# Head pair 0's K and V made during the layer norm of the keys, with other PSUM banks for Q and a norm cut into eight units

## The chip, the cores and the metric

The kernel runs on all 8 cores of one Trainium2 chip. Two cores share one of the 4 batch entries; each of the two owns half of its 4096 query rows and reads all 4096 key rows. No core sends anything to another. The metric is the device time of the slowest core in microseconds (us).

## The reference

All of it for x of shape [4, 4096, 1024], 16 heads of 64 columns, and a feed-forward layer with 3072 hidden columns and int weights:

```python
xn = _layernorm(x)
q = split_heads(xn @ Wq) + pos; k = split_heads(xn @ Wk) + pos; v = split_heads(xn @ Wv)
scores = einsum('bhqd,bhkd->bhqk', q, k) / sqrt(1024)     # causal mask, then softmax
s = (softmax(scores) @ v, heads merged) @ Wo
g = silu(down(silu(gate(xn)) * up(xn)))                    # weights int * 1/127
out = x + s * g
```

## The kernel before

The program is written engine by engine. `P.op` (line 142) appends one operation to the list of its engine, with the semaphore counts that it waits for; `P.flush` (line 150) closes a block. Each engine carries out its own list strictly in the order of the calls, so the order in which Python emits operations is the order on every engine. The engines are T (TensorE), V (VectorE), S (ScalarE), G (GpSimd, which issues the weight loads) and SY (SyncE, which issues the x loads). DVE in the profile is VectorE, ACT is ScalarE.

The blocks are: b0, the layer norm of the own query rows; f1 and f2, the feed-forward layer; b34, the layer norm of the 32 key tiles of 128 rows and the Q projection; b5, K, V and attention for 8 pairs of heads; b6, the output projection. The change touches b34 and b5.

**b34.** `ln_phase` (line 270) handles tile n as a chain. VectorE sums x (line 301), ScalarE squares it (304), VectorE sums the squares (307), small operations follow on both (310 to 328), and VectorE writes the normed tile (332). TensorE transposes it with 8 matmuls (347) and ScalarE copies the result into `xn_kv` (354). Then `interleave_cb(n)` may emit other work, which lies in every engine's list ahead of tile n+1. In the kernel before, `b4_cb` (627) emits the Q projection of pair p, `emit_qpair(p)` (575), after tile n = 16 + 2p. It has four groups, one for each 512 query rows: 8 matmuls into `Qps` (595, two banks in turn), position added (602), square (607), a matmul with a column of ones into `SQp1` (611), and a maximum over it (619). A group's ones matmul lies in TensorE's list ahead of the next group's 8 matmuls.

**b5.** `kv_units(p)` (687) returns the preparation of pair p as 43 units: one that issues the loads of Wk and Wv (696, 701); 8 K units, `emit_kg` (8 matmuls at 715, evacuated at 723, banks `KVp[0]` and `KVp[1]` in turn); one norm unit, `u_norms`, which goes over all 8 groups of K with one scratch buffer `sSQ` (square 740, ones matmul 747, maximum 753, running maximum 763); 32 V units, `emit_vc` (8 matmuls at 779 for 128 keys, evacuated at 787); and `u_bound` (798), which turns the maxima into the exponential's bias `sBM` (VectorE 800 to 810, matmul 816, VectorE 825). Pair 0's units are all emitted ahead of its attention (965).

`attention(p)` (837) has four query blocks j with 8, 16, 24 and 32 key chunks c. Chunk c is: two matmuls into `SC2[c % 2]` (851), one exponential of 128 x 1024 on ScalarE (865), for the last 4 chunks of a block two multiplications with the triangle (878), and, emitted two chunks later, two matmuls into `AVps` (897). After every odd chunk, and once after the block's last AV matmuls, one unit of pair p+1 is taken from the list `fillers` (911, 915). I call these places slots: 5 + 9 + 13 + 17 = 44 in a pair. What is left in the list is emitted after the last block (962). At the end of a block ScalarE inverts the sums (922, 929), TensorE spreads them into `KVp` (936), and VectorE copies them (945) and scales the output (953).

Of the kernel before, what the change touches and what calls it, by code (L numbers as in the profile page):

```python
# [172 lines left out]
def build_program(cfg):  # L173
# [40 lines left out]
    with ExitStack() as top:  # L214
        P.mksem(top, "sT", "sS", "sV", "dC", "dX0", "dX1", "dW0", "dW1",
                "dS0", "dS1", "dG0", "dG1", "dR0", "dR1", "dR2", "dR3", "dO0", "dO1", "dP", "dK")
# [11 lines left out]
        b5set = 2 * S + 2 * KVC * 130 + 4 * EC * 128 + 2 * 2 * QBS + 512 + QBS  # L228
# [15 lines left out]
        o = 0  # L244
# [10 lines left out]
        sSQ = BIG1[:, o:o + 512]  # L255
        o += 512
# [13 lines left out]
        def ln_phase(xt_src, ntile, xn_dst, dsem, gates, tag, pool_ext=None,  # L270
                     xnt_ext=None, xnt_gate=None,
                     tp_gate=None, sq_gate=None, interleave_cb=None):
            with ExitStack() as ph:
# [3 lines left out]
                else:  # L277
# [5 lines left out]
                Tps = [pe(nc.psum_tensor(f"Tps{tag}{i}", [128, GT * 128], F32))  # L283
                       for i in range(2)]
                sqb = pe(nc.psum_tensor(f"sqb{tag}", [128, E], F32))
# [8 lines left out]
                for n in range(ntile):  # L294
# [64 lines left out]
                    if interleave_cb is not None:  # L359
                        interleave_cb(n)  # L360
                return last_ev, tile_toks

        with ExitStack() as phb0:
# [178 lines left out]
            with ExitStack() as phc:  # L542
# [3 lines left out]
                sPQ = Kp[0][:, 0:OWN]  # L546
# [17 lines left out]
                with ExitStack() as ph4:  # L564
                    p4 = ph4.enter_context
                    Qps = [p4(nc.psum_tensor(f"Qps{i}", [128, QW], F32))
                           for i in range(2)]
                    SQp1 = p4(nc.psum_tensor("SQp1", [1, QW], F32))
                    wq_free = [None, None]
                    qps_free = [None, None]  # L570
                    b4st = dict(sqmm_free=None, sqb_free=tok_f2T)
                    tok_mq = [None] * NP
                    qbs_per_qs = max(1, 4 // NQW)

                    def emit_qpair(p):
                        par = p % 2
                        dsem = "dS0" if par == 0 else "dS1"
                        tw = P.op("G", lambda g, o=Wsl[par][:],
                                  s=wqr[:, :, p * 128:(p + 1) * 128]:
                                  g.dma_start(out=o, in_=s),  # L580
                                  waits=[wq_free[par], tok_f2T], inc=dsem, amt=16)
                        rlast = None
                        for qs in range(NQW):
                            qp = qs % 2
                            last = None
                            for ec in range(EC):
                                w = [tw, tok_xnown, qps_free[qp]]
                                if p == 0 and qs == 0 and ec == 0:
                                    w += [tok_f2S, tok_f1V]
                                last = P.op(  # L590
                                    "T", lambda t, o=Qps[qp][:],
                                    l=Wsl[par][:, ec, :],
                                    r=xn_own[:, ec, qs * QW:(qs + 1) * QW],
                                    st=(ec == 0), sp=(ec == EC - 1):
                                    t.matmul(o, l, r, start=st, stop=sp),
                                    waits=w, inc="sT" if ec == EC - 1 else None)
                            wq_free[par] = last
                            tev = P.op("V", lambda v,
                                       o=Q_all[:, p, qs * QW:(qs + 1) * QW],
                                       a=Qps[qp][:],  # L600
                                       b=sPQ[:, qs * QW:(qs + 1) * QW]:
                                       v.tensor_tensor(o, a, b, ALU.add),
                                       waits=[last, tpq], inc="sV")
                            qps_free[qp] = tev
                            tsq = P.op("V", lambda v, o=sSQ[:, 0:QW],
                                       a=Q_all[:, p, qs * QW:(qs + 1) * QW]:
                                       v.tensor_tensor(o, a, a, ALU.mult),
                                       waits=[tev, b4st["sqb_free"]], inc="sV")
                            tmm = P.op("T", lambda t, o=SQp1[0:1, 0:QW],
                                       l=sONE[:], r=sSQ[:, 0:QW]:  # L610
                                       t.matmul(o, l, r, start=True, stop=True),
                                       waits=[tsq, tok_consts,
                                              b4st["sqmm_free"]], inc="sT")
                            b4st["sqb_free"] = tmm
                            for jj in range(qbs_per_qs):
                                j = qs * qbs_per_qs + jj
                                rlast = P.op(
                                    "V", lambda v, p=p, j=j, jj=jj:
# [8 lines left out]
                    def b4_cb(n):  # L627
                        if n >= 16 and (n - 16) % 2 == 0 and (n - 16) // 2 < NP:
                            emit_qpair((n - 16) // 2)
# [453 lines left out]
```

How the kernel before makes its waits and increments, by code:

```python
            def body(eng):  # L152
                hw = self.hw[qn]
                for fn, waits, inc, amt in ops:
                    for (sn, val) in waits:
                        if val > hw.get(sn, 0):
                            eng.wait_ge(self.sems[sn][0], val)
                            hw[sn] = val
                    ins = fn(eng)
                    if inc is not None:
                        ins.then_inc(self.sems[inc][0], amt)
```

## Time and profile before

| | |
|---|---|
| median of 3 runs | 2590.89 us (2503.78 to 2601.6) |
| profiled execution, its own time | 2503.69 us |
| its span, first to last instruction | 2502.1 us |
| spans of the 8 cores in it | 2495.4 to 2502.1 us |
| TensorE (PE) busy | 1716.1 us, 69% |
| VectorE (DVE) busy | 827.2 us, 33% |
| ScalarE (ACT) busy | 956.7 us, 38% |
| b34, from the first key tile's load | 752 to 1114 us |
| K and V of pair 0 ahead of the attention | 1114 to 1180 us |
| attention of 8 pairs | 1180 to 2353 us |
| output projection | 2353 to 2502 us |

A timeline row gives the start in us from the span's start, the length in us, the engine, the line and the operation; in brackets stands how long the engine had been idle before it and whose result ended that. PEld rows (weight loads) lie beside the PE rows. The granted clock is 1.0 at 2.4 GHz and 0.5 at 1.2 GHz.

### The profile page before, as it was taken

The numbers are of one execution on the slowest core, as the hardware profiler recorded it, in microseconds if no ns is written. First come the engines' busy times: TensorE is split into PE (matmuls) and PEld (weight loads), VectorE is DVE, ScalarE is ACT, GpSimd is POOL, SyncE is SP. The second block draws the span as 40 slices with busy tenths as digits, with TensorE's granted clock in tenths as the row PEclk, the third lists the DMA queues.
The fourth block names the chain that finished last, engine by engine and source line by source line (L and its number), as shares of the span: only waits on it lengthen the run. The fifth ranks groups of instructions, "written<-read, shape, count | busy, mean of one in ns | idle before, by whom it ended". The sixth has DMA issues, their size and how long they took to land. (4 is left out here: it accounts for less than half of the span.)

```text
span 2502.1 us, 26111 instructions; the slowest of 8 cores (2495.4 to 2502.1 us)
## 1 busy us (share of the span) xinstructions
PE 1716.1 (69%) x8995; PEld 706.8 (28%) x9088; DVE 827.2 (33%) x1746; ACT 956.7 (38%) x1125; POOL 87.4 (3%) x135
## 2 busy tenths in 40 slices
PE   1178888989991144437787787878877697776753
PEld 0134444444440111114232232323222232221221
DVE  4533333330005544434413323232332423321133
ACT  3311111111003311110485675747657475677500
POOL 0011101000000000000000000000000000000000
PEclk9999999999995576678898888978888888888886
DMA  2153433320114221220000000000000000020155
GB/s 77 59 64 39 51 39 45 44 26 30 54 52 109 76 51 42 42 33 10 5 1 9 1 5 5 5 5 1 5 5 5 1 1 1 1 34 1 51 176 176
DMA packets 75135, 89.85 MB, mean 36 GB/s; under 512 B 52994, under 2 KB 53122, under 8 KB 74882
## 3 DMA queue, kind: packets, MB, share of 16 engines
q0 software_dynamic: 62768, 45.62, 11.7%
q1 hardware_dynamic: 12242, 42.57, 5.3%
q8 instruction: 77, 1.26, 0.2%
q14 instruction: 48, 0.39, 0.1%
HBM read 100.24 MB, written 16.78 MB: 47 GB/s over the span
## 5 line engine op out<-in xcount | busy, mean ns | idle before, releaser
L865 ACT ACTIVATE BIG<-SC,sBM 128x1024 bf16<-128x1024 f32 x640 | 681.9, 1110 | 343.7 <-PE SC L851 343.2
L897 PE MATMUL AVps<-BIG 128*65 128x512 bf16 x1280 | 425.6, 414 | 87.3 <-DVE BIG L878 42.0
L851 PE MATMUL SC<-BIG 64*128 64x512 bf16 x1280 | 265.0, 420 | 0.0
L485 ACT ACTIVATE sSG<-Gps 128x512 bf16<-128x512 f32 x96 | 57.3, 597 | 378.5 <-PE Gps L471 378.5
L787 DVE CAST BIG<-KVp 128x128 bf16<-128x128 f32 x256 | 75.0, 293 | 375.1 <-PE KVp L779 372.3
L471 PE MATMUL Gps<-RA,wgT 128*128 128x512 bf16 x752 | 195.5, 405 | 1.4 <-issue 0.7
L481 PE MATMUL Ups<-RA,wuT 128*128 128x512 bf16 x744 | 180.6, 382 | 1.3
L779 PE MATMUL KVp<-BIG 128*128 128x128 bf16 x2048 | 167.8, 230 | 13.5 <-DVE BIG L945 13.1
L897 PEld LDWEIGHTS AVps<-BIG 128*65 128x65 bf16 x1280 | 104.4, 114 | 235.2 <-issue 224.5
L347 PE MATMUL Tpsb<-sID,BIG 128*128 128x128 bf16 x256 | 32.4, 306 | 200.1 <-DVE BIG L332 200.1
L525 PE MATMUL Dps<-BIG 128*128 128x512 bf16 x752 | 165.1, 379 | 2.2 <-PEq L164 1.4
L490 DVE TENSOR_TENSOR BIG<-sSG,Ups 128x512 bf16<-128x512 bf16 x96 | 66.0, 687 | 283.5 <-PE Ups L481 279.0
L878 DVE TENSOR_TENSOR BIG<-BIG,sTRI 128x512 bf16<-128x512 bf16 x256 | 97.3, 421 | 174.8 <-ACT BIG L865 174.8
L779 PEld LDWEIGHTS KVp<-BIG 128*128 128x128 bf16 x2048 | 126.0, 102 | 77.4 <-issue 73.5
L715 PE MATMUL KVp<-BIG 128*128 128x512 bf16 x489 | 131.3, 415 | 23.3 <-DMA BIG<-Wv 11.0
L851 PEld LDWEIGHTS SC<-BIG 64*128 64x128 bf16 x1280 | 59.7, 94 | 268.2 <-issue 268.2
L471 PEld LDWEIGHTS Gps<-RA,wgT 128*128 128x128 bf16 x768 | 77.5, 102 | 94.4 <-issue 16.4
L322 ACT ACTIVATE sLN<-sLN,sCV 128x1 f32<-128x1 f32 x48 | 14.1, 294 | 235.0 <-DVE sLN L319 235.0
L481 PEld LDWEIGHTS Ups<-RA,wuT 128*128 128x128 bf16 x768 | 76.2, 99 | 95.0 <-issue 7.8
L525 PEld LDWEIGHTS Dps<-BIG 128*128 128x128 bf16 x768 | 75.1, 98 | 92.2 <-issue 1.8
L1025 PE MATMUL OPs<-BIG,RA 128*128 128x512 bf16 x250 | 71.4, 450 | 37.7 <-DVE ot L1042 33.3
L747 PE MATMUL KVp<-BIG,sONE 128*1 128x512 bf16 x64 | 32.6, 510 | 90.1 <-DVE BIG L740 90.1
(79 smaller groups left out, 1292.9 us busy)
## 6 DMA issues: line engine op xcount, KB each, us to landing
xstA<-x_q SPq DMA_DIRECT2D x32, 512.0 KB, 4.4
xstb<-x_kv SPq DMA_DIRECT2D x32, 512.0 KB, 3.6
g_spill<-xstA POOLq DMA_DIRECT2D x16, 512.0 KB, 2.9
gt<-g_spill POOLq DMA_DIRECT2D x16, 512.0 KB, 6.0
out<-ot SPq DMA_DIRECT2D x16, 512.0 KB, 3.0
wgc<-wg POOLq DMA_DIRECT2D x24, 256.0 KB, 4.1
wuc<-wu POOLq DMA_DIRECT2D x24, 256.0 KB, 5.6
wdc<-wd POOLq DMA_DIRECT2D x24, 256.0 KB, 5.7
```

The lines of the kernel that those rows point to most:

```text
L471: t.matmul(o, l, r, start=st, stop=sp),
L481: t.matmul(o, l, r, start=st, stop=sp),
L490: v.tensor_tensor(o, a, b, ALU.mult),
L525: t.matmul(o, l, r, start=st, stop=sp),
L715: t.matmul(o, l, r, start=st_, stop=sp),
L779: t.matmul(o, l, r, start=st_, stop=sp),
L787: v.tensor_copy(o, i_),
L851: t.matmul(SC2[bi][:, h * QBS:(h + 1) * QBS], Kp[par][h * 64:(h + 1) * 64, c * 128:(c + 1) * 128], Q_all[h * 64:(h + 1) * 64, p, j * QBS:( ...
L865: s.activation(expb[bi], SC2[bi][:], AF.Exp, scale=cfg.SM, bias=sBM[par][:, col:col + 1]),
L878: v.tensor_tensor(expb[bi][:, h * QBS:(h + 1) * QBS], expb[bi][:, h * QBS:(h + 1) * QBS], sTRI[:, r * QBS:(r + 1) * QBS], ALU.mult),
L897: t.matmul(AVps[h][:], Vaug[par][:, c, h, :], expb[bi][:, h * QBS:(h + 1) * QBS], start=st_, stop=sp),
L1025: t.matmul(OPs[op][:, ew * EW:(ew + 1) * EW], AO[:, rc, q2 * 128:(q2 + 1) * 128], Wo_sb[:, rc, ew * EW:(ew + 1) * EW], start=st_, stop=sp),
```

## The change

1. The PSUM tensors of attention (`SC2`, `AVps`, `KVp`) are now allocated ahead of b34. b34 uses them: the transposes go to `SC2[1]`, the squares of the layer norm to `AV2`, the Q matmuls to the first bank of `SC2[0]`, the Q ones matmul to its second. So Q has one bank instead of two, and it is marked free only after the maximum (619 before).
2. Q of pair p is emitted after tile 2p instead of 16 + 2p.
3. The units of pair 0 are emitted inside b34, each after the tile that completes its input: the loads after tile 0, V unit c after tile c, K unit g and the norm of its group after tile 4g + 3, the bound at the end. The callback emits at most three units for one tile. Pair 0's weights go to slices 2 and 3 of `Wsl`, so that they don't collide with Wq.
4. `u_norms` is cut into 8 units, and `sSQ` has two halves. With one empty unit, `u_setk`, a pair has 1 + 8 + 1 + 8 + 32 + 1 = 51 units instead of 43. The loop over slots is as before.
5. K/V loads count on semaphores of their own (`dV0`, `dV1`), and `sPQ` lies in another part of `Kp[1]`.

```diff
-                sPQ = Kp[0][:, 0:OWN]
+                sPQ = Kp[1][:, 2 * E:2 * E + OWN]
...
+                Qps = [SC2[0][:, 0:QW]]
+                SQp1 = SC2[0][0:1, 512:512 + QW]
...
+                        qp = 0
...
+                        b4st["sqmm_free"] = rlast
+                        qps_free[qp] = rlast
...
+                def kv_units(p, ks, vs, xw):
...
+                    units.append((0, u_dma))
...
+                    for kg_ in range(NKG):
+                        units.append(((kg_ + 1) * TPK - 1,
+                                      lambda kg_=kg_: emit_kg(kg_)))
...
+                    units.append((NKG * TPK - 1, u_setk))
+
+                    def u_norm1(kg):
+                        sqi = kg % 2
+                        tsq = P.op("V", lambda v, sqi=sqi,
+                                   o=sSQ[sqi][:, 0:KW],
+                                   a=Kp[par][:, kg * KW:(kg + 1) * KW]:
+                                   v.tensor_tensor(o, a, a, ALU.mult),
+                                   waits=[st["kvb"][kg % 2],
+                                          sqst["free"][sqi], kv["ktok"]],
+                                   inc="sV")
...
+                    for kg_ in range(NKG):
+                        units.append(((kg_ + 1) * TPK - 1,
+                                      lambda kg_=kg_: u_norm1(kg_)))
...
+                    for c_ in range(KVC):
+                        units.append((c_, lambda c_=c_: emit_vc(c_)))
...
+                    units.append((KVC - 1, u_bound))
...
+                b34q = [(2 * p_, lambda p_=p_: emit_qpair(p_))
+                        for p_ in range(NP)]
+                holder = {}
+                b34q += kv_units(0, 2, 3, lambda r: holder["toks"][r])
+                b34q.sort(key=lambda it: it[0])
...
+                def b34_cb(n, toks):
+                    holder["toks"] = toks
+                    c = 0
+                    while (qpos[0] < len(b34q) and b34q[qpos[0]][0] <= n
+                           and c < 3):
+                        b34q[qpos[0]][1]()
+                        qpos[0] += 1
+                        c += 1
...
+                    tps_ext=[SC2[1][:, 0:GT * 128],
+                             SC2[1][:, GT * 128:2 * GT * 128]],
+                    sqb_ext=AV2[:, 0:E],
...
-                    for u in kv_units(0):
-                        u()
                     for p in range(NP):
                         if p + 1 < NP:
-                            fillers.extend(kv_units(p + 1))
+                            fillers.extend(
+                                fn for _, fn in kv_units(
+                                    p + 1, (p + 1) % 2, 2 + (p + 1) % 2,
+                                    lambda r: tok_xnkv))
                         attention(p)
```

## Rows read from the trace of the kernel before

**Rows 1.** The page's granted clock in 40 slices, and its costliest group
```profile
PEclk9999999999995576678898888978888888888886
...
L865 ACT ACTIVATE BIG<-SC,sBM 128x1024 bf16<-128x1024 f32 x640 | 681.9, 1110 | 343.7 <-PE SC L851 343.2
```

**Rows 2.** Timeline, one layer-norm tile: start us, length us, engine, line, operation, [idle before]
```profile
826.30 1.01 PE L347 MATMUL Tpsb<-sID,BIG 128*128 128x128 bf16 x8 [5.90 <-DVE BIG L332]
826.98 1.07 ACT L354 CAST BIG<-Tpsb 128x512 bf16<-128x512 f32 x2 [2.24 <-PE Tpsb L347]
...
829.09 1.23 DVE L307 TENSOR_REDUCE sLN<-sqbb 128x1 f32<-128x1024 f32 x1 [1.91 <-ACT sqbb L304]
...
833.21 1.01 PE L347 MATMUL Tpsb<-sID,BIG 128*128 128x128 bf16 x8 [5.90 <-DVE BIG L332]
```

**Rows 3.** Timeline of the Q projection: two groups at the higher clock, one at the lower
```profile
880.45 1.90 PE L595 MATMUL Qps<-RA,BIG 128*128 128x512 bf16 x8
880.62 0.68 DVE L619 TENSOR_REDUCE sMQ<-SQp 1x1 f32<-1x512 f32 x1 [0.63 <-PE SQp L611]
...
892.28 1.20 DVE L301 TENSOR_REDUCE sLN<-xstb 128x1 f32<-128x1024 f32 x1
...
970.77 3.20 PE L595 MATMUL Qps<-RA,BIG 128*128 128x512 bf16 x8
```

**Rows 4.** Tile 0: timeline row of its transposes, and the Wq loads of line 580
```profile
763.95 1.01 PE L347 MATMUL Tpsb<-sID,BIG 128*128 128x128 bf16 x8 [17.51 <-DVE BIG L332]
...
L580 POOL DMA_DIRECT2D BIG<-Wq x8: 873/873/901, 754.0 to 1043.4; - x8
...
DMA to landing us min/median/max: 4.2/4.6/19.1
```

**Rows 5.** Timeline from the last layer-norm tile to the first attention exponential
```profile
1112.80 1.07 ACT L354 CAST BIG<-Tpsb 128x512 bf16<-128x512 f32 x2 [2.17 <-PE Tpsb L347]
...
1124.18 2.72 PE L715 MATMUL KVp<-BIG 128*128 128x512 bf16 x6 [11.04 <-DMA BIG<-Wv]
...
1127.64 0.69 DVE L723 TENSOR_TENSOR BIG<-KVp,sPK 128x512 bf16<-128x512 f32 x1 [15.78 <-PE KVp L715]
...
1156.26 20.28 PE L779 MATMUL KVp<-BIG 128*128 128x128 bf16 x256
...
1176.86 0.21 DVE L800 TENSOR_SCALAR sMK<-sMQ,sMK 1x4 f32<-1x4 f32 x1
...
1179.52 1.28 ACT L865 ACT_TABLE_LOAD   x1 [65.65 <-DVE sBM L825]
```

**Rows 6.** Timeline of the norm unit that lies in the attention of pair 2
```profile
1517.58 2.12 ACT L865 ACTIVATE BIG<-SC,sBM 128x1024 bf16<-128x1024 f32 x2 [1.34 <-PE SC L851]
...
1521.58 0.41 DVE L740 TENSOR_TENSOR BIG<-BIG 128x512 bf16<-128x512 bf16 x1
...
1522.13 0.38 PE L747 MATMUL KVp<-BIG,sONE 128*1 128x512 bf16 x1 [1.59 <-DVE BIG L740]
1522.68 0.68 DVE L753 TENSOR_REDUCE sMK<-KVp 1x1 f32<-1x512 f32 x1 [0.70 <-PE KVp L747]
...
1535.00 1.11 ACT L865 ACTIVATE BIG<-SC,sBM 128x1024 bf16<-128x1024 f32 x1 [15.30 <-PE SC L851]
...
1536.54 1.11 ACT L865 ACTIVATE BIG<-SC,sBM 128x1024 bf16<-128x1024 f32 x1 [0.42 <-PE SC L851]
```

**Rows 7.** Timeline: an ordinary stretch of slots, a masked chunk, the end of a pair
```profile
1610.18 2.12 ACT L865 ACTIVATE BIG<-SC,sBM 128x1024 bf16<-128x1024 f32 x2 [0.19 <-PE SC L851]
...
1621.57 0.76 DVE L878 TENSOR_TENSOR BIG<-BIG,sTRI 128x512 bf16<-128x512 bf16 x2 [0.25 <-ACT BIG L865]
...
1626.54 0.24 PE L816 MATMUL KVp<-sBSB,sOR 1*128 1x1 bf16 x4 [3.14 <-DVE sBSB L810]
...
1632.08 1.40 DVE L945 CAST BIG<-KVp 64x512 bf16<-64x512 f32 x2 [4.50 <-PE KVp L936]
1632.67 2.12 ACT L865 ACTIVATE BIG<-SC,sBM 128x1024 bf16<-128x1024 f32 x2 [1.44 <-PE SC L851]
```

More of the change, by code:

```diff
@@ L254, in build_program @@
         o += 2 * 2 * QBS
-        sSQ = BIG1[:, o:o + 512]
-        o += 512
+        sSQ = [BIG1[:, o:o + 512], BIG1[:, o + 512:o + 1024]]
+        o += 1024
         sRS = BIG1[:, o:o + QBS]
@@ L271, in ln_phase @@
                      xnt_ext=None, xnt_gate=None,
-                     tp_gate=None, sq_gate=None, interleave_cb=None):
+                     tp_gate=None, sq_gate=None, interleave_cb=None,
+                     tps_ext=None, sqb_ext=None):
             with ExitStack() as ph:
@@ L282, in ln_phase @@
                         for i in range(2)]
-                Tps = [pe(nc.psum_tensor(f"Tps{tag}{i}", [128, GT * 128], F32))
-                       for i in range(2)]
-                sqb = pe(nc.psum_tensor(f"sqb{tag}", [128, E], F32))
+                Tps = tps_ext if tps_ext is not None else [
+                    pe(nc.psum_tensor(f"Tps{tag}{i}", [128, GT * 128], F32))
+                    for i in range(2)]
+                sqb = sqb_ext if sqb_ext is not None else pe(
+                    nc.psum_tensor(f"sqb{tag}", [128, E], F32))
                 xst_free = [None, None]
@@ new lines, in build_program @@
+                SC2W = max(2 * QBS, 2 * GT * 128, 2 * QW)
+                SC2 = [pc(nc.psum_tensor(f"SC2_{i}", [128, SC2W], F32))
+                       for i in range(2)]
+                AVPD = max(QBS, 512)
+                KVPD = max(KW, 512)
+                AV2 = pc(nc.psum_tensor("AV2", [128, max(2 * AVPD, E)], F32))
+                KV2 = pc(nc.psum_tensor("KV2", [128, max(2 * KVPD, E)], F32))
+                AVps = [AV2[0:65, 0:QBS], AV2[0:65, AVPD:AVPD + QBS]]
+                KVp = [KV2[:, 0:KW], KV2[:, KVPD:KVPD + KW]]
@@ new lines, in build_program @@
+                tok_xnkv, _ = ln_phase(
+                    xkv_t, ntile_kv, xn_kv, ("dX0", "dX1"),
+                    [tok_f1T, tok_f1V], "b",
+                    xnt_ext=[Kp[1][:, i * E:(i + 1) * E]
+                             for i in range(2)],
+                    xnt_gate=tok_f2T,
+                    tp_gate=tok_f2S, sq_gate=tok_f1V,
+                    tps_ext=[SC2[1][:, 0:GT * 128],
+                             SC2[1][:, GT * 128:2 * GT * 128]],
+                    sqb_ext=AV2[:, 0:E],
+                    interleave_cb=b34_cb)
@@ L655, in build_program @@
+                while qpos[0] < len(b34q):
+                    b34q[qpos[0]][1]()
+                    qpos[0] += 1
+                tok_b4T = P.cnt("sT")
+                tok_b4V = P.cnt("sV")
+                tok_b4S = P.cnt("sS")
+                P.flush("b34")
                 tok_Q = tok_b4V
+                st["sc2"] = [tok_Q, tok_b4S]
+                st["av_free"] = [tok_Q, tok_Q]
+                st["sl_free"][0] = tok_b4T
+                st["sl_free"][1] = tok_b4T
                 with ExitStack() as ph5:
```

467 lines of the change are left out of this document (214 added, 253 removed).

## The prediction

> **What bounds the kernel now.** I read the page first. ScalarE's exponential is the costliest group and ScalarE waited 344 us for the scores, so in attention ScalarE is starved at some places; and the granted clock falls to 0.5 for two slices and stays at 0.6 to 0.7 for four more, from the key layer norm to the start of attention [rows 1]. Then I read timelines of single periods, because the two blocks have different limits.
>
> In b34 nothing is busy enough to be the limit: a plain tile takes 6.91 us (transposes at 826.30 and at 833.21) and is one chain over three engines. The sum of squares (line 307) starts at 829.09, and the chain runs on from there; ahead of it TensorE and VectorE have gaps [rows 2]. In attention a slot of two chunks keeps ScalarE idle for only 0.19 us per 2.12 us of exponentials [rows 7]. One unit breaks this: the norm unit. Each of its 8 groups is square, ones matmul, maximum in turn through one scratch buffer; TensorE stands in it, no scores come, and ScalarE is idle for 15.3 us [rows 6]. It occurs in 7 pairs' attention. Ahead of attention K and V of pair 0 run alone: from the last copies' end (1112.80 + 1.07 = 1113.87) to the first exponential (1179.52 + 1.28 = 1180.80) it is 66.9 us, 11.0 of them a wait for Wv [rows 5].
>
> **The change in b34.** Emission order is execution order, so what a unit makes VectorE wait for lies ahead of tile n+1's sums.
>
> Removed: the 66.9 us, less what must still follow tile 31. That is K group 7 (start to evacuation 3.5 us, evacuation 0.7 [rows 5]), its square 0.4, ones matmul to maximum 0.6, maximum 0.7 [rows 6], V unit 31 with evacuation 1.2, and the bound from 1176.86 to 1180.80, 3.9 [rows 5]. With hand-overs about 11.5 us. Gain 55.
>
> Tile 0: Q of pair 0 now follows tile 0. Its matmuls would start at about 765.2; but Wq, issued at 754.0 behind the loads of the positions, landed after 19.1 us, at 773.1 [rows 4]. Cost 8 us. Sixteen tiles of layer norm covered this before. Bounds 0 (if it lands as the median load, 4.6 us) and 12 (if Wk and Wv, now behind it, slow it down).
>
> One Q bank: group q+1 started at 880.45, while the maximum of group q ran from 880.62 to 881.30 [rows 3]. Now it starts behind the maximum, at about 881.4: 0.93 us later, three times in a pair, 8 pairs: 22 us. The longer gap also bears on the clock. The same 8 matmuls took 1.90 us at 2.4 GHz and 3.20 at 1.2 GHz [rows 3]; a slow group moves what follows by 1.5 us. Of 24 later groups 3 were slow before. I take 1.3 more in each pair, 8 x 2 = 16 us; bounds 0 and, if all are slow, 36.
>
> V units: in 16 tiles with nothing else (n = 1, 5, ... and the even ones from 16) the copies end at 828.05 [rows 2]. The V unit takes 8 matmuls at 1.2 GHz, to about 829.1, and its evacuation 0.3, to 829.45. The sum of x, 1.2 us long [rows 3], used to lie beside the transposes and now comes after, and the sum of squares starts at 830.55 instead of 829.09: 1.45 us each, 23 us. Bounds 0 (if VectorE had room) and 35. In the 8 Q tiles only the end of the V unit sticks out behind the last maximum, 0.5 us: 4.
>
> K units with their norm, 7 tiles (the eighth is in the tail above): K matmuls from 828.15, evacuation at 831.7, square from 832.5, maximum 833.7 to 834.4, V unit evacuated by 834.9 or, where V waits for the bank of that maximum (odd groups), 835.8. The sum of squares starts at 836.0 or 836.9, 6.9 or 7.8 late: 51 us.
>
> Sum for b34: 8 + 22 + 16 + 23 + 4 + 51 - 55 = +69 us.
>
> The Trainium skill (page "TensorE: Matmul & The Clock Gate", on engine queue depths) says that ScalarE and VectorE are strict first-in first-out and that only TensorE lets weight loads pass. The trace agrees: in Q tiles the sum of x starts only at 892.28, behind the last maximum. If VectorE could pass a waiting evacuation, the V and K terms, 78 us, would go; that is the second rival below.
>
> **The change in attention**, for each of the 7 pairs with fillers.
>
> The norm unit goes: 15.3 us of idle, less the 0.19 of an ordinary slot, plus 0.7 because the next exponentials came 1.54 us apart instead of 1.1 while the clock recovered [rows 6, 7]: -15.8.
>
> Eight norm units take slots 11 to 18, which had V units. The square of the next group can run while TensorE does other chunks, so most cost nothing. Three are different. In slots 12 and 13 (masked chunks 13 and 15 of block 1) the square lies behind the mask of the same chunk, which starts about 1.6 us after the exponentials' pair and lasts 0.76 [rows 7]: TensorE waits, and the AV matmuls behind it come about 1.7 and 1.2 us later. In slot 15 the square lies behind copies and scalings of 1.40 us each: 1.3. Less 0.5 for the V units that were there: +3.7. Bounds 0 and 8.
>
> The bound left slot 43, where TensorE waited 3.14 us [rows 7]; a V unit is there now (20.28 us for 32, 0.63 each [rows 5]), and a part of the wait lay beside masks: -2.1.
>
> Fifty-one units don't fit in 44 slots. Six V units and the bound are left and come after the pair, with ScalarE idle, since the next pair's exponentials need the bias. The V units wait for `KVp`, copied from 1632.08 to 1633.48; six units and their first evacuation behind the scalings take until 1638.8; the bound without its table load 2.7: 1641.5, against an exponential at 1632.67 [rows 5, 7]. 8.9, less 0.8 as the first AV matmul no longer waits for the scaling: +8.1. If the clock is low, 10 or 11.
>
> Sum: -15.8 + 3.7 - 2.1 + 8.1 = -6.1 us, seven times: -43. Bounds -9 and -3 each: -63 and -21. Pair 1's Wk and Wv are issued only after b34, but their first use is some 7 us later and a load takes about 5: nothing, at most 4.
>
> **Sum.** +69 - 43 = +26 us on the profiled execution's 2503.7 (span 2502.1): about 2530 us. That execution is at the low end of the three runs, whose median is 2590.9; I predict on its footing. About 2% (50 us, so 2454 to 2554) is what a measurement of this kernel can tell from no change.
>
> **Rivals.**
>
> *The clock stays low (slower).* If every gap of some 2.5 us drops TensorE to 1.2 GHz, all later Q groups are slow (+20 over my sum) and the end of each pair runs slow (+3 x 7): 2573 us. For it: one pair's second group was slow with gaps of only 1.8 us, and the layer norm runs at 0.5 [rows 1, 3]. Against: most groups with such gaps ran at 1.90. It decides from two slow groups a pair on. The Trainium skill has a rule that speaks for it (the same page, "A second HAM failure mode: psum-queue depth-cycling"): small idles between matmul groups that wait for PSUM make the clock swing, and throughput falls.
>
> *The layer norm hides the units (faster).* If VectorE's gaps in b34 take in the evacuations, the 78 us go and -50 remains: 2452 us. For it: VectorE and TensorE are mostly idle there. Against: list order, and the 892.28 row. It decides if over 75 of the 78 go.
>
> *The norm units stall anyway (slower).* If each of the 8 stands 1.9 us for its square, 15 us a pair, attention gains nothing: +11.3 x 7 on my sum, 2609 us. Against: a square takes 0.41 us and VectorE is idle in unmasked slots.
>
> **Chances.** Forecast, within 2%: 0.70. Low clock 0.18, stalls 0.05: slower 0.23. Hidden units 0.07: faster. The range takes the bounds: the Q clock 0 to 36, the V units, and -63 to -21 for attention. The low ends seldom meet: 2494 to 2575.
>
> **What would show it.** Right: layer-norm tiles of 8.4 us with V only and about 14 with K; Q of pair 0 starting at about 773; ones matmuls at even spacing in the slots and no 15 us idle of ScalarE; 8 to 9 us idle of it at each pair's end; first exponential near 1250 instead of 1181; pair periods 6 us shorter. Wrong: V-only tiles still at 6.9, or norm units with TensorE waits of over 1 us in unmasked slots.

## The result, and the profile after

| | kernel before | changed kernel |
|---|---|---|
| median | 2508.12 us (8 runs) | 2574.55 us (8 runs, 2572.91 to 2577.23) |
| ratio of the times | | 1.0274, 95% interval 1.0262 to 1.0287 |
| spans of the 8 cores in the profiled execution | 2495.4 to 2502.1 us | 2561.1 to 2575.5 us |
| TensorE (PE) busy | 69% | 69% |
| core 0: transposes of tile 0 to those of tile 31 | 759.7 to 1108.0 us | 763.75 to 1254.78 us |
| core 0: first and last exponential | 1175.3, 2345.5 us | 1269.33, 2419.7 us |
| core 0: attention between them | 1170.3 us | 1150.4 us |

The change costs 2.7%. The forecast was 1% more and "within 2%". From here on all rows and numbers are of core 0, unless another core is named. It is the slowest core of the changed kernel; before it was the fastest one, and core 6, whose rows the prediction used, the slowest. So the change is 80.1 us on core 0 (2495.4 to 2575.5), 62.0 us on core 6 (2502.1 to 2564.1) and 66.4 us between the medians: differences of core 0 overstate it. In some executions the cores of one die ran at a lower granted clock and took some per cent longer; the ratios in this document leave these out, and so do the times of "norm in one unit" and "pair 0's K and V behind", of which two executions each are left.

The page of the changed kernel, its granted clock in 40 slices of 64.4 us and its costliest group:

```profile
PEclk9999999999985655555589798888889788888886
...
L903 ACT ACTIVATE BIG<-SC,sBM 128x1024 bf16<-128x1024 f32 x640 | 683.9, 1111 | 321.8 <-PE SC L889 257.5
```

TensorE stood at or near 0.5 from slice 13 to slice 20, which is from 773 to about 1290 us, where before only two slices stood at 0.5 [rows 1]. In attention ScalarE waits less, 321.8 us instead of 342.4 (core 0 of before). So the attention gained and b34 lost, as forecast; the sizes differ. The windows view of b34, before and changed (its columns: the stretch, its length, the busy time and the number of instructions of PE, PEld, DVE, ACT and POOL, the granted clock, the DMA share, GB/s):

```profile
759.70:1108.00 348.30, 116.69 (x529) 53.00 (x538) 174.97 (x344) 77.57 (x155) 5.24 (x6) 0.66 0.22 53
...
763.00:1255.00 492.00, 207.78 (x837) 89.70 (x851) 195.94 (x404) 77.61 (x155) 5.24 (x6) 0.55 0.17 39
```

The granted clock is 0.55 where it was 0.66. Timeline rows of two layer-norm tiles of the changed kernel, one with a V unit only, one with a K unit, its norm and a V unit:

```profile
804.53 1.01 PE L350 MATMUL SC<-sID,BIG 128*128 128x128 bf16 x8 [5.38 <-DVE BIG L335]
...
807.54 0.29 DVE L772 CAST BIG<-KV 128x128 bf16<-128x128 f32 x1 [3.16 <-PE KV L765]
807.75 1.21 DVE L304 TENSOR_REDUCE sLN<-xstb 128x1 f32<-128x1024 f32 x1
...
812.82 1.01 PE L350 MATMUL SC<-sID,BIG 128*128 128x128 bf16 x8 [5.38 <-DVE BIG L335]
...
1137.95 1.01 PE L350 MATMUL SC<-sID,BIG 128*128 128x128 bf16 x8 [5.38 <-DVE BIG L335]
...
1151.80 1.01 PE L350 MATMUL SC<-sID,BIG 128*128 128x128 bf16 x8 [6.07 <-DVE BIG L335]
```

Transposes to transposes it is 8.29 us with V only (6.91 before, [rows 2]) and 13.85 us with K. The list order of VectorE is to be read at 807.54: the evacuation of the V unit waits for TensorE, and the sum of x (line 304) starts only behind it, though ScalarE began to square the same x at 806.17, 1.6 us earlier. Timeline rows of Q groups, the first in tile 0 and others:

```profile
772.80 3.57 PE L605 MATMUL SC<-RA,BIG 128*128 128x512 bf16 x8 [8.04 <-DMA BIG<-Wq]
...
778.61 0.68 DVE L631 TENSOR_REDUCE sMQ<-SC 1x1 f32<-1x512 f32 x1 [0.84 <-PE SC L623]
...
779.43 3.57 PE L605 MATMUL SC<-RA,BIG 128*128 128x512 bf16 x8 [0.93 <-DVE sMQ L631]
...
875.74 1.89 PE L605 MATMUL SC<-RA,BIG 128*128 128x512 bf16 x8 [0.93 <-DVE sMQ L631]
...
900.60 3.44 PE L605 MATMUL SC<-RA,BIG 128*128 128x512 bf16 x8 [0.93 <-DVE sMQ L631]
```

Q of pair 0 starts at 772.80, behind an 8.04 us wait for Wq. In every later group of a pair TensorE stands idle for 0.93 us, from the ones matmul to the end of the maximum. One of these groups, at 875.74, took 1.89 us. The others shown took 3.57 and 3.44; of the 24 later groups 23 took 2.69 us or more. The median of one matmul is 631 ns where it was 380. The groups view of TensorE between 763 and 1256 us (count, busy us, mean ns of one matmul, idle us before them and who ended it):

```profile
L605 PE MATMUL SC<-RA,BIG 128*128 128x512 bf16 x248 | 104.4, 594 | 31.2 <-DVE sMQ L631 22.3 <-DMA BIG<-Wq 8.0 <-issue 0.9
...
L623 PE MATMUL SC<-BIG,sONE 128*1 128x512 bf16 x32 | 16.4, 514 | 49.1 <-DVE BIG L618 49.1
```

The same view of before has 74.3 us, 452 ns and 1.8 us of idle time for its Q matmuls. So the Q matmuls took 30.1 us more, waited 22.3 us for the maxima and 8.0 us for Wq. Timeline rows from the last tile to the attention:

```profile
1254.78 1.01 PE L350 MATMUL SC<-sID,BIG 128*128 128x128 bf16 x8 [5.38 <-DVE BIG L335]
...
1269.33 2.12 ACT L903 ACTIVATE BIG<-SC,sBM 128x1024 bf16<-128x1024 f32 x2
...
1278.21 3.57 PE L688 MATMUL KV<-BIG 128*128 128x512 bf16 x8 [4.52 <-DMA BIG<-Wv]
```

14.55 us lie between the last tile's transposes and the first exponential, where before it was 67.3 (1108.0 to 1175.3). The first K unit of the attention then waits 4.52 us for Wv, and ScalarE, behind it, is idle for 8.37 us. Timeline rows of three of the eight norm units of one pair:

```profile
1609.19 0.42 DVE L716 TENSOR_TENSOR BIG<-BIG 128x512 bf16<-128x512 bf16 x1
...
1609.76 0.38 PE L723 MATMUL KV<-BIG,sONE 128*1 128x512 bf16 x1 [2.56 <-DVE BIG L716]
...
1611.25 1.11 ACT L903 ACTIVATE BIG<-SC,sBM 128x1024 bf16<-128x1024 f32 x1 [2.83 <-PE SC L889]
...
1615.25 0.58 PE L723 MATMUL KV<-BIG,sONE 128*1 128x512 bf16 x1 [2.56 <-DVE BIG L716]
...
1624.75 0.59 PE L723 MATMUL KV<-BIG,sONE 128*1 128x512 bf16 x1 [2.64 <-DVE BIG L716]
...
1626.97 1.11 ACT L903 ACTIVATE BIG<-SC,sBM 128x1024 bf16<-128x1024 f32 x1 [3.07 <-PE SC L889]
...
1632.67 0.38 PE L723 MATMUL KV<-BIG,sONE 128*1 128x512 bf16 x1
```

The norm matmuls of slots 12, 13 and 15 wait 2.56, 2.56 and 2.64 us for their squares, and ScalarE stands idle for 2.83 and 3.07 us behind the first and the third; behind the second it waits in front of the block's end, which these rows do not show. Slots 12 and 13 lie beside masked chunks, slot 15 behind the copies and scalings of the block before. The one at 1632.67, in a slot with neither, waits for nothing. Timeline rows of two pairs' ends:

```profile
1412.71 4.80 PE L765 MATMUL KV<-BIG 128*128 128x128 bf16 x48 [1.72 <-DVE BIG L984]
...
1420.44 2.12 ACT L903 ACTIVATE BIG<-SC,sBM 128x1024 bf16<-128x1024 f32 x2 [10.07 <-PE SC L889]
...
1567.04 2.12 ACT L903 ACTIVATE BIG<-SC,sBM 128x1024 bf16<-128x1024 f32 x2 [10.12 <-DVE sBM L810]
```

Six V units in one go (48 matmuls, 4.80 us), then the bound, and ScalarE idle for 10.07 us where it was 1.44 [rows 7]. The pair's period is 1567.04 - 1420.44 = 146.60 us; before it was 150.2 (seven pairs in 1051.4 us; now in 1031.3).

### The profile page after: what moved, and what is told of

It is laid out like the page before. It is cut to its first block and busy times, and to the rows that moved or that the text cites. A ratio compares the mean times of both kernels' runs of the same rounds, so it can differ in the third digit from the quotient of the medians.

```text
span 2575.5 us, 26000 instructions; the slowest of 8 cores (2561.1 to 2575.5 us)
## 1 busy us (share of the span) xinstructions
PE 1779.6 (69%) x8992; PEld 730.4 (28%) x9088; DVE 828.8 (32%) x1746; ACT 958.9 (37%) x1125; POOL 87.4 (3%) x135
## 5 line engine op out<-in xcount | busy, mean ns | idle before, releaser
L903 ACT ACTIVATE BIG<-SC,sBM 128x1024 bf16<-128x1024 f32 x640 | 683.9, 1111 | 321.8 <-PE SC L889 257.5
L936 PE MATMUL AV<-BIG 128*65 128x512 bf16 x1280 | 422.0, 413 | 86.6 <-DVE BIG L917 36.3
L765 PE MATMUL KV<-BIG 128*128 128x128 bf16 x2048 | 182.8, 245 | 37.1 <-DVE BIG L984 19.0
L772 DVE CAST BIG<-KV 128x128 bf16<-128x128 f32 x256 | 75.2, 294 | 362.3 <-PE KV L765 361.7
L936 PEld LDWEIGHTS AV<-BIG 128*65 128x65 bf16 x1280 | 102.9, 115 | 239.8 <-issue 230.0
L765 PEld LDWEIGHTS KV<-BIG 128*128 128x128 bf16 x2048 | 141.6, 110 | 97.7 <-issue 94.5
L688 PE MATMUL KV<-BIG 128*128 128x512 bf16 x486 | 145.9, 450 | 25.0 <-ACT BIG L357 9.0
L350 PE MATMUL SC<-sID,BIG 128*128 128x128 bf16 x256 | 32.4, 306 | 185.4 <-DVE BIG L335 185.4
L605 PE MATMUL SC<-RA,BIG 128*128 128x512 bf16 x248 | 104.4, 594 | 31.2 <-DVE sMQ L631 22.3
L695 DVE TENSOR_TENSOR BIG<-KV,sPK 128x512 bf16<-128x512 f32 x64 | 44.2, 690 | 191.9 <-PE KV L688 191.8
```

The costliest lines, as they stand in the source:

```text
L688: t.matmul(o, l, r, start=st_, stop=sp),
L765: t.matmul(o, l, r, start=st_, stop=sp),
L772: v.tensor_copy(o, i_),
L903: s.activation(expb[bi], SC2[bi][:, 0:2 * QBS], AF.Exp, scale=cfg.SM, bias=sBM[par][:, col:col + 1]),
L936: t.matmul(AVps[h][:], Vaug[par][:, c, h, :], expb[bi][:, h * QBS:(h + 1) * QBS], start=st_, stop=sp),
```

## Experiments

All ran beside the kernel before. "First exponential" is its start, "attention" the time from there to the start of the last exponential, both on core 0 of the profiled execution.

| kernel | median us | ratio to before, 95% interval | first exponential us | attention us |
|---|---|---|---|---|
| changed kernel | 2574.55 | 1.0274 (1.0262 to 1.0287) | 1269.3 | 1150.4 |
| Q bank freed earlier | 2504.75 | 0.998 (0.994 to 1.001) | 1196.6 | 1144.6 |
| gaps filled | 2531.28 | 1.008 (1.004 to 1.012) | 1222.0 | 1145.8 |
| norm in one unit | 2598.5 | 1.034 (1.024 to 1.044) | 1268.1 | 1174.2 |
| seven more slots | 2515.39 | 1.002 (0.999 to 1.005) | 1265.5 | 1084.2 |
| pair 0's K and V behind | 2537.0 | 1.013 (1.011 to 1.016) | 1230.6 | 1148.7 |
| norm units moved | 2527.91 | 1.009 (1.008 to 1.011) | 1262.7 | 1102.8 |
| all three repairs | 2412.80 | 0.963 (0.961 to 0.965) | 1206.4 | 1055.8 |
| b34 laid out anew | 2208.91 | 0.882 (0.880 to 0.884) | 1006.9 | 1047.1 |

### The wait for the maximum, and the clock

One line is taken out, so that the Q bank is free again once its sum has been evacuated. This is what the changed kernel's first release already said; the second one overwrote it.

```diff
-                        qps_free[qp] = rlast
```

> The changed kernel with one line less: the Q bank is free after the evacuation and no longer only after the maximum. In the changed kernel 1 of 24 later Q groups ran its 8 matmuls in 1.9 us; the others took 2.7 to 3.6. Theory A (the 0.93 us wait also keeps the clock low): the wait goes, 24 x 0.93 = 22 us, and most later groups return to 1.9 us, another 20 to 30: 45 us less than the changed kernel, about 2530. Theory B (the clock is low for another reason, such as the V units or the early place of Q): only 22 us go, about 2552, and the groups stay at 3 us and more.

The groups view of TensorE in b34, and then timeline rows, both of this kernel:

```profile
L605 PE MATMUL SC<-RA,BIG 128*128 128x512 bf16 x248 | 71.3, 437 | 5.5 <-DMA BIG<-Wq 4.9 <-issue 0.4
...
L623 PE MATMUL SC<-BIG,sONE 128*1 128x512 bf16 x32 | 12.2, 383 | 48.5 <-DVE BIG L618 48.5
```

```profile
872.47 1.90 PE L605 MATMUL SC<-RA,BIG 128*128 128x512 bf16 x8
872.64 0.68 DVE L631 TENSOR_REDUCE sMQ<-SC 1x1 f32<-1x512 f32 x1 [0.63 <-PE SC L623]
...
876.15 1.90 PE L605 MATMUL SC<-RA,BIG 128*128 128x512 bf16 x8
```

The group at 872.47 now starts 0.17 us ahead of the maximum, right behind the ones matmul, instead of after 0.93 us of idle TensorE, and takes 1.90 us; so do 23 of the 24 later groups. The Q matmuls take 71.3 us instead of 104.4, the 32 ones matmuls 12.2 instead of 16.4, and no time goes into waiting for maxima. The granted clock of b34 is 0.66, as before the change. Sum: 33.1 + 4.2 + 22.3 = 59.6 us; another 6 come from shorter V matmuls (27.5 instead of 30.4 us) and Wq (4.9 instead of 8.0). The tiles span 423.2 us instead of 491.0, 67.8 less. One line is thus worth 70 us of the total, more than I had expected (45), since the clock took more than I had put down for it. Theory B is out: the early place of Q and the V units are as before, and the groups are fast.

The same wait with no idle time in it tells whether the wait itself or TensorE's idleness brings the low clock. This kernel adds matmuls whose result is not used: four between a Q group and its ones matmul, three between that and the next group.

```diff
                         sqi = qs % 2
+                        for _d in range(4):
+                            P.op("T", lambda t: t.matmul(
+                                KVp[1][:, 0:KW], sID[:], xn_own[:, 0, 0:KW],
+                                start=True, stop=True), waits=[...])
```

> The changed kernel, its waits kept, with 4 matmuls of 128 x 512 ahead of each Q ones matmul and 3 behind it; their results are not used (they go to a K/V bank that is free then). They fill TensorE's gaps of 1.47 and 0.93 us. Theory A (low clock because of idle gaps): later groups run in 1.9 us, the wait of 0.93 stays, 25 to 33 us less than the changed kernel, about 2545. Theory B (the groups are slow for another reason, such as the PSUM bank or the loads): groups stay slow and the added matmuls make it 0 to 20 us longer.

Timeline rows of this kernel:

```profile
876.69 1.03 PE L622 MATMUL KV<-RA,sID 128*128 128x512 bf16 x4
...
878.64 0.82 PE L633 MATMUL KV<-RA,sID 128*128 128x512 bf16 x3
...
879.64 1.89 PE L605 MATMUL SC<-RA,BIG 128*128 128x512 bf16 x8 [0.18 <-DVE sMQ L641]
```

TensorE now waits only 0.18 us at the maximum, and the next group takes 1.89 us. All Q matmuls take 69.0 us. All 24 later groups now take 1.89 us, and the granted clock of b34 is 0.69. The dependency is the same, and TensorE does 61 us more work in b34 (35.0 and 26.3 us for the added matmuls), yet the first exponential comes 47 us earlier. So the low clock came from the idle gaps, not from the wait on the bank as such. This kernel fills both gaps of a group, 1.47 us ahead of the ones matmul and 0.93 behind it; that the second alone makes the difference is shown by the kernel before this one, which has the first gap and fast groups.

### The units inside the layer norm

Pair 0's units, all but the loads, are emitted behind the layer norm again. Q stays as in the changed kernel.

```diff
-                b34q += kv_units(0, 2, 3, lambda r: holder["toks"][r])
-                b34q.sort(key=lambda it: it[0])
+                kv0 = [fn for _, fn in
+                       kv_units(0, 2, 3, lambda r: holder["toks"][r])]
+                b34q.insert(1, (0, kv0.pop(0)))
...
+                for fn in kv0:
+                    fn()
```

> The changed kernel with pair 0's K and V units emitted behind the layer norm, as in the kernel before, all but their two loads, which stay ahead (issued behind tile 0). Everything else of the change stays (one Q bank, the attention's units). The layer norm stage loses the V units of its 16 tiles without a Q pair (1.4 us each, 22 us), the 4 us of those that share a tile with a Q pair, and 7 K tiles at 7.2 us (51 us): 77 us. Behind it the units take what they took before, 66.9 us from the end of the layer norm, less about 11 us of waiting for Wv, which is now there, and less some 11 us of units that were in the tail anyway: 44 us. Theory A (units emitted into the layer norm delay it by nearly their own time, because VectorE goes through one list): the first exponential comes about 33 us earlier than in the changed kernel, near 1236 us on core 0, total near 2541. Rival (the units lie hidden inside the layer norm and the loss is all the Q groups'): the first exponential comes about 44 us later, near 1313, total near 2618.

Timeline rows of this kernel, the last tile and the first exponential:

```profile
1172.08 1.01 PE L350 MATMUL SC<-sID,BIG 128*128 128x128 bf16 x8 [5.90 <-DVE BIG L335]
...
1230.62 2.12 ACT L906 ACTIVATE BIG<-SC,sBM 128x1024 bf16<-128x1024 f32 x2
```

The tiles span 1172.08 - 760.3 = 411.8 us. Against the changed kernel's 491.0 the V and K units cost 79.2 us inside the layer norm; the sum had 78. Against the 348.3 of before, Q alone costs 63.5 us; the sum had 46. Behind the tiles it is 58.5 us to the first exponential. The kernel took 2534.07 and 2539.93 us, against 2541 expected. The rival (units hidden in the layer norm) had 2618 and is out. So placing the units in the tiles loses time by itself: 79.2 us of delay for 58.5 - 14.55 = 44 us saved behind. With the loads issued early, K and V behind the tiles take 58.5 us, 8.8 less than before. The Q groups are slow here too (23 of the 24 later ones took more than 2.5 us, granted clock 0.57), with no V or K unit in the layer norm.

### The norm units and the masks

The norm is one unit again in pairs 1 to 7 (43 units), so nothing is left over at a pair's end.

```diff
+                    def u_norms():
+                        u_setk()
+                        for kg in range(NKG):
+                            u_norm1(kg)
```

> The changed kernel, but for pairs 1 to 7 the norm is one unit again (43 units in 44 slots, nothing left behind the pair); pair 0 in the layer norm is as changed. It gives the net price of the attention part by itself. By the rows of the changed kernel a pair period is 146.6 us against 150.2 before: expected 3.6 x 7 = 25 us more than the changed kernel, about 2600. The rival, that the left-over units eat all that the cut norm gave, expects no difference, about 2575.

One timeline row shows it, the exponential behind the norm unit:

```profile
1474.92 1.11 ACT L912 ACTIVATE BIG<-SC,sBM 128x1024 bf16<-128x1024 f32 x1 [15.65 <-PE SC L898]
```

ScalarE is idle for 15.65 us here and for 15.30 in the other six pairs, as in [rows 6]; the attention takes 1174.2 us, 23.8 more than in the changed kernel (25 were expected) and 4 more than before. The rival, no difference, is out. Cutting the norm was right, and its gain of 20 us was what was left of more than 100 (7 x 15.8) after the costs in the slots, at the pairs' ends and at the first pair's wait for Wv. The next two kernels take two of these away.

Here only the order of the units differs. The first norm stays in slot 11, four V units take slots 12 to 15 (12 and 13 beside masks, 14 at the block's end, 15 behind its copies), and seven norms follow in slots 16 to 22.

```diff
+                            nm, vc = un[10:18], un[18:50]
+                            fillers.extend(un[:10] + nm[:1] + vc[:4]
+                                           + nm[1:] + vc[4:] + un[50:])
```

> The changed kernel with another order of the units in the attention: the first norm unit stays in slot 11, four V units take slots 12 to 15, the other seven norm units take slots 16 to 22, which lie at the first query block after the one whose chunks are masked; the number of units and slots is the same. In the changed kernel three norm units lie in slots beside masked chunks, and ScalarE stood idle for 5.9 us more there than with V units in these slots; norms in the unmasked slots cost nothing that the trace shows. Theory A (a norm matmul waits 2.6 us for VectorE only where the masks stand ahead of its square): about 5 us less for each of 7 pairs, the attention 35 us shorter, total near 2540. Rival (the norm's wait costs wherever it is placed): no change within 5 us.

Timeline rows of this kernel, two pairs' first exponentials and, between them, one norm unit:

```profile
1403.73 2.12 ACT L903 ACTIVATE BIG<-SC,sBM 128x1024 bf16<-128x1024 f32 x2 [10.00 <-DVE sBM L810]
...
1460.11 0.41 DVE L716 TENSOR_TENSOR BIG<-BIG 128x512 bf16<-128x512 bf16 x1
...
1461.58 0.38 PE L723 MATMUL KV<-BIG,sONE 128*1 128x512 bf16 x1
...
1463.06 2.12 ACT L903 ACTIVATE BIG<-SC,sBM 128x1024 bf16<-128x1024 f32 x2 [0.15 <-PE SC L889]
...
1543.57 2.12 ACT L903 ACTIVATE BIG<-SC,sBM 128x1024 bf16<-128x1024 f32 x2 [10.10 <-PE SC L889]
```

The norm matmul at 1461.58 has no wait, and the next exponential comes after 0.15 us. This pair's period is 139.84 us instead of 146.60, and the attention is 47.6 us shorter; 35 were expected. Taken from exponential to exponential and over the periods 2 to 7, a period is 6.2 us shorter on average (140.5 against 146.7), and all of it lies in the three stretches behind slots 12, 13 and 15 (1.7, 3.3 and 1.2 us), while slot 16, which now has a norm, takes 0.6 us more. The first period is 10.1 us shorter, 3.0 of that because its wait for Wv is 1.56 us here and not 4.52. The mean granted clock of the attention is 0.89 here and 0.86 in the changed kernel, but outside of the slots named no stretch of two chunks changed by more than 0.4 us, and the end of the pair is unchanged (10.10 us idle). So the higher mean clock bought almost no time elsewhere.

### The units left over at the end of a pair

Seven slots more in block 3, after chunks 2, 6, ..., 26. All 51 units then fit.

```diff
-                                if c % 2 == 1 and fillers:
+                                if (c % 2 == 1 or (j == 3 and c % 4 == 2
+                                                   and c < 28)) and fillers:
```

> The changed kernel with 7 more slots in query block 3 (after chunks 2, 6, ... 26), so that all 51 units have a place and none is left behind the pair. Theory A (the tail costs 8 us a pair, and a V unit in a slot of block 3 0.2 to 0.4 us): 8.1 less 2 = 6 us a pair, 7 x 6 = 42 us less than the changed kernel, about 2533. Theory B (TensorE is already full there, a V unit costs its whole 0.6 us and the exponentials slip further): under 20 us less, over 2555.

Timeline rows, the first exponential of two pairs in a row:

```profile
1406.80 2.12 ACT L903 ACTIVATE BIG<-SC,sBM 128x1024 bf16<-128x1024 f32 x2 [1.44 <-PE SC L889]
...
1543.64 2.12 ACT L903 ACTIVATE BIG<-SC,sBM 128x1024 bf16<-128x1024 f32 x2 [1.44 <-PE SC L889]
```

ScalarE is idle for 1.44 us at the pair's end instead of 10.07, and the period is 1543.64 - 1406.80 = 136.84 us, 9.8 less. The attention is 66.2 us shorter, where 42 were expected. Taken from exponential to exponential, over the periods 2 to 7, the end of a pair gives 8.9 us, and each of the six stretches of block 3 in which an additional slot shows costs 0.3 us, 1.8 together: both as theory A had it. What it did not have is 2.5 us in three stretches near the starts and ends of blocks. One of them is the start of block 1. There a K unit's 8 matmuls took 3.41 us in the second pair of the changed kernel (at 1440.37) and take 1.89 here (at 1426.97), so the clock is part of it; the granted clock of the attention is 0.89 here too. But the same unit took 3.30 us in the kernel before as well, where nothing was left over at a pair's end, so the left-over units are not its only cause, and why it is fast here is open.

### Together, and a better layout

All three repairs: the line of the first experiment out, norms in unmasked slots, and 49 units (the loads merged with the first K unit, the empty unit with the last) in 49 slots.

```diff
-                        qps_free[qp] = rlast
...
+                                if (c % 2 == 1 or (j == 3 and c % 4 == 2
+                                                   and c < 20)) and fillers:
...
+                                [lambda un=un: (un[0](), un[1]())] + kg[1:7]
+                                + [lambda un=un: (un[8](), un[9]())]
+                                + nm[:3] + vc[:4] + nm[3:] + vc[4:] + un[50:])
```

> The changed kernel with its three costs taken out together: the line that made each Q group wait for the last maximum is removed, so the Q groups run with one bank but without that wait; the norm units lie in slots without masks; and the 52 units are made 49 by merging the loads with the first K unit, with 5 more slots in the last query block, so that no unit is left for the end of the pair. From the runs so far: 70 us from the first, 60 us from more slots, 35 us from the norms' place (expected, being measured beside this run). Theory A (the three are separate and add up): 2575 - 165 = 2410 us, first exponential near 1197, attention near 1060 us on core 0. Rival (the attention is bound elsewhere once the idle times at its end are gone, so that the second and third overlap): attention near 1085 us, total near 2440.

2412.8 us against 2410 expected, and 1055.8 us of attention where 1060 were expected. But the sum of the expectation had 35 us for the norms' place, which by itself gave 47. By what each repair gave by itself (69.8, 59.2 and 46.6 us between the medians) it should have been 176 us, and it is 162: the three nearly add up, and the hit is in part luck. (The expectation's 52 units are 51.) The first exponential comes at 1206.4, where 1197 were expected, and the first pair waits 7.51 us for Wv. With these repairs the change makes the kernel 3.7% faster instead of 2.7% slower.

Last, the tile and its guests are interleaved by engine. A callback between ScalarE's two small activations and VectorE's normalising emits the V unit of tile n - 1 with its evacuation, the ones matmul of a Q group with its maximum, and the matmuls of the next Q group; a second one behind the normed tile emits the evacuation and the square of Q. One Q group per tile replaces four in every second one of the first 16. This kernel also issues the Wq loads two pairs ahead and pair 1's Wk and Wv before the attention, so it is not an experiment on one thing.

```diff
+                    if mid_cb is not None:
+                        mid_cb(n, tile_toks)
                     t10 = P.op("V", ...)
                     t11 = P.op("V", ...)
+                    if post_cb is not None:
+                        post_cb(n)
...
+                def mid_cb(n, toks):
+                    if n >= 1:
+                        un0[18 + n - 1]()
+                    if n >= 2:
+                        q_ones(n - 2)
+                    if n >= 1:
+                        q_mm(n - 1)
+                def post_cb(n):
+                    if n >= 1:
+                        q_ev(n - 1)
```

> The attention is that of the kernel with the three costs taken out. The layer norm stage is laid out anew: instead of a Q pair of four groups in every second tile, each tile carries one Q group and one V unit, and every fourth one K group, whose matmuls are emitted ahead of the tile's transposes while their VectorE work is emitted behind them, so that TensorE has matmuls while VectorE normalises, and VectorE waits for no product. Per tile TensorE has 8 transposes, 8 matmuls of 512 columns (1.9 us), 8 of 128 columns and one of 512 for the sum: well under the 6.85 us that VectorE takes; VectorE has its 6.85 us, two evacuations and a square and a maximum, about 2.5 us, and in every fourth tile as much again. Theory A (the stage is bound by VectorE's own work): 32 tiles at 9.4 to 10.5 us and 15 us at its end, the first exponential 1020 to 1060 us on core 0 instead of 1269, total near 2250 (with an attention as in the kernel above). Rival (TensorE's granted clock falls to half in these thinner tiles, and the groups take 3.6 us and the transposes twice their time): tiles of 13 us, first exponential near 1150, total near 2360.

Timeline rows of one tile of this kernel:

```profile
984.10 0.61 PE L354 MATMUL SC<-sID,BIG 128*128 128x128 bf16 x8 [0.63 <-DVE BIG L337]
...
985.80 0.61 PE L776 MATMUL KV<-BIG 128*128 128x128 bf16 x8 [1.09 <-ACT BIG L361]
...
986.64 1.90 PE L612 MATMUL SC<-RA,BIG 128*128 128x512 bf16 x8
986.69 1.23 DVE L310 TENSOR_REDUCE sLN<-AV 128x1 f32<-128x1024 f32 x1 [0.47 <-ACT AV L307]
...
988.51 0.29 DVE L783 CAST BIG<-KV 128x128 bf16<-128x128 f32 x1
...
989.68 0.81 DVE L337 TENSOR_SCALAR BIG<-xstb,sLN 128x1024 bf16<-128x1024 f32 x1
990.41 0.69 DVE L625 TENSOR_TENSOR BIG<-SC,BIG 128x512 bf16<-128x512 f32 x1
...
990.64 0.61 PE L354 MATMUL SC<-sID,BIG 128*128 128x128 bf16 x8 [2.10 <-DVE BIG L337]
```

While VectorE sums the squares (986.69) TensorE runs the Q group; the evacuation of Q stands behind the normed tile and waits for nothing, and that of the V unit (988.51) stands behind the small operations and waits for nothing either. This tile takes 6.54 us, with a V unit and a Q group in it, where the bare tile took 6.91 [rows 2]. The 32 tiles span 227.8 us (762.85 to 990.64) instead of 491, 7.35 a tile on average; the granted clock of the stretch is 0.80. The first exponential comes at 1006.9, better than the 1020 to 1060 expected, and the total is 2208.9 us, 11.8% below the kernel before. Theory A's price of 9.4 to 10.5 us a tile was too high: it took the bare tile's whole period, 6.85 us, for VectorE's own work, while all of VectorE's work in this stretch is 187 us, 5.8 a tile. The rival (clock at half in thin tiles) is out as a whole, though not everywhere: some Q groups still took 3.19 us. How much of the gain is the order of the lists and how much the clock was not taken apart.

## Why the prediction was wrong, step by step

The sign of both halves was right. The sum was too small by 40 us: 26 us forecast, 66 us measured between the medians. It was put together on core 6's rows. On core 6 the change is 62.0 us: the tiles and what follows up to the first exponential +86.5 (forecast +69), the attention -24.9 (forecast -43), the rest 0.5. On core 0, from which the table is, these are +90.0 and -19.9, and 10 us more lie outside of both blocks (4.1 ahead of tile 0, 5.9 in b6).

| term | predicted us | measured us | by |
|---|---|---|---|
| tile 0 waits for Wq | 8 | 8.0 | groups view |
| one Q bank, waits | 22 | 22.3 | groups view, Q bank freed earlier |
| one Q bank, clock | 16 | 30.1, and some 4 in the ones matmuls | groups view, gaps filled |
| V and K units in the tiles | 78 | 79.2 | pair 0's K and V behind |
| removed ahead of attention | -55 | -52.8 | 67.3 to 14.55 |
| seven pairs of attention | -43 | -20.1 | 1051.35 to 1031.3 |

**What bounds the kernel, and b34's chain.** Right. The list order of VectorE, which the waits at 807.54 show and the Trainium skill states (page "TensorE: Matmul & The Clock Gate", on engine queue depths), cost what the rows of before said it would: 8.29 us a tile with V (8.4 forecast), 13.85 with K (about 14). The rival of hidden units had this one thing against it, and it fell.

**The clock term: this step failed.** I counted the slow groups of before (3 of 24) and added 1.3 to each pair, 16 us; it measured 34. The groups of before started right behind the ones matmul, 0.17 us ahead of the maximum, and the new ones after 0.93 us of idle TensorE. The one gave 3 slow groups of 24, the other 23, and with the gap filled none was slow: the share of before said nothing about a gap that was longer. A group that is slow from end to end takes 3.57 us, not the 3.20 of the row I used. The upper bound of this term (36, all slow) was nearly reached, and the rival "the clock stays low" had the total, 2573 us (its own terms give 2571), in part by luck: its slow ends of pairs were not what the attention lost. The rival's turning point, two slow groups a pair, was passed by one. The rule that stood for it in the Trainium skill (page "TensorE: Matmul & The Clock Gate", section "A second HAM failure mode: psum-queue depth-cycling") describes what the two Q experiments measured: with waits for the bank 104.4 us of Q matmuls, without them 71.3. I had set the majority of groups of before against it, at gaps that the change was about to lengthen. A chance of 0.18 was too low for this.

**The attention: two more terms failed.** Here the periods 2 to 7 of before and of the changed kernel are set side by side, from exponential to exponential, on core 0. The norm unit's removal gave 15.9 us a pair (forecast 15.8). The norm slots cost 5.9, not 3.7: 1.7 behind slot 12 (as forecast), 2.8 behind slot 13 (1.2 forecast) and 1.4 behind slot 15 (1.3 forecast, and 0.5 had been taken off for the V units). The left-over units and the bound's new place together cost 6.3 us (forecast 8.1 - 2.1 = 6.0), though ScalarE's stop of 10 us looks larger. So a period is 3.5 us shorter, not 6.1. The first period is 1.1 us longer than before and not 6.1 shorter: the wait for Wv, put at nothing, "at most 4", was 4.52 us on TensorE and 8.37 on ScalarE. Six times 2.6 and once 7.2 us are the 23 us that are missing. The wait for Wv differs from kernel to kernel (1.08 us with seven more slots, 1.56 with the norms moved, 7.51 with all three repairs), so its size here is one execution's.

**The range and the chances.** 2494 to 2575 holds the 2574.55 by its last half microsecond. The bounds that it names add up to more: 20, 12 and 22 us over the sum for the Q clock, the V units and the attention, 2584. "Within 2%" at 0.70 was wrong: it needed the clock and the attention to be near their middles at once, when both erred to the same side. Of the signs that it gave, the tiles of 8.4 and 14 us, Q at 773 and no stop of 15 us came true; the stops at the pairs' ends were 10 us and not 8 to 9, and one norm matmul waited over 1 us in a slot without masks (slot 15, 2.64 us), which the prediction had also named as an exception.

**Open.** Why the repair of one line gave 6 us more than its own groups was traced to V matmuls and Wq in one execution only. The 5.9 us that b6 took longer on core 0 of the changed kernel (155.8 against 149.9) was not seen on core 6 (150.5 against 149.6); the other cores lie between -1.1 and +4.7. It was not tested. Why the norm in slot 13 costs 2.8 us, when it waits as long as the one in slot 12, was not tested either.

## What to carry to other kernels

Look where moved work will stand in the list of every engine. In this kernel an evacuation emitted ahead of the next tile's first operation made the tile 1.4 us longer, and with the evacuations at places where their products were ready the tile was no longer than a bare one. When a change puts a wait between groups of matmuls, price the groups at the lower clock throughout and see whether the forecast still holds. Cutting a long unit into slots pays only as far as there are slots for the pieces, and a slot where the unit's VectorE work stands behind a mask or a copy is not free (5.9 us a pair here). To learn what a change cost, compare the kernels stretch by stretch between the same events; the idle time at one row can be time that was lost elsewhere before.

## What the runs showed of the hardware that I had not expected

- With 0.93 us of idle TensorE ahead of each later group of 8 matmuls (128x512), behind a first gap of 1.47 us, 23 of 24 groups took 2.69 to 3.57 us and the stage's granted clock was 0.55; without the 0.93 us, 23 of 24 took 1.9 us and the clock was 0.66. Taking out that wait won 70 us of 2575.
- 224 matmuls (128x512) whose results nobody reads, put into the gaps, cost 61 us of TensorE's time and made the kernel 43 us faster.
- Moving the norm units out of slots 12 to 15 raised the mean granted clock of 1100 us of attention from 0.86 to 0.89, and so did taking the 10 us stop out of each pair's end. With the norms moved, the stretches outside of the slots concerned did not get shorter by more than 0.4 us each.
